# Moving one of seven products behind two other blocks of TensorE work in 19 quads of a gated attention layer

## The reference

```python
x = x + tanh(g_xattn) * attention(layernorm(x), ctx)
n = layernorm(x)                                   # 2048 tokens x 512
scores = softmax(n @ gate_w.T)                     # 64 experts
w_e    = top-8 of scores, the rest 0
flat   = w_e[:, inv_map]                           # 8 groups x 8
scalar = flat.sum(-1)
soft   = softmax(where(flat == 0, -1e9, flat), -1)
xg = n[:, None, :] + einsum('ngi,ghi->ngh', soft, mask_up_w)
g  = einsum('ngh,gih->ngi', xg, gate_proj_w)       # inner size 352 per group
u  = einsum('ngh,gih->ngi', xg, up_proj_w)
d  = einsum('ngi,ghi->ngh', silu(g) * u, down_proj_w)
x  = x + tanh(g_ffn) * einsum('ng,ngh->nh', scalar, d)
```

## Time and profile before

| | us |
|---|---|
| median of 3 runs | 1065.21 |
| lowest and highest of them | 1064.68, 1065.55 |
| the profiled execution | 1064.01 |
| its span in the profile | 1062.2 |

### The profile page before, as it was taken

How to read it: one execution, slowest core, us unless ns; L and a number is a source line. 1 busy time by engine, 2 the same in 40 slices (tenths; PEclk the granted TensorE clock), 3 DMA queues, 4 the chain that set the end, 5 groups by cost and what they waited for, 6 DMA issues and landing times.

```text
span 1062.2 us, 14524 instructions
## 1 busy us (share of the span) xinstructions
PE 1046.7 (99%) x5394; PEld 889.4 (84%) x5394; DVE 747.4 (70%) x1315; ACT 389.5 (37%) x651; POOL 615.6 (58%) x545
## 2 busy tenths in 40 slices
PE   8999999999999999999999999999999999999998
PEld 8889988988988778888887888888888888888887
DVE  7874655676678788788789888765666665666655
ACT  5334324334434434243424342333333333332331
POOL 2112102122435976768878987778668677668661
PEclk9999999999999999999999999999999999999999
DMA  9112225256786314123236332593321211221202
GB/s 335 73 40 99 61 50 149 62 135 144 238 251 198 118 36 56 66 77 35 95 107 81 121 104 97 170 296 114 114 75 48 75 59 44 75 74 48 75 28 80
DMA packets 114277, 111.64 MB, mean 105 GB/s; under 512 B 20896, under 2 KB 96672, under 8 KB 114208
## 3 DMA queue, kind: packets, MB, share of 16 engines
q1 hardware_dynamic: 113840, 110.58, 35.7%
q10 hardware_dynamic: 368, 0.15, 0.1%
HBM read 79.05 MB, written 31.65 MB: 104 GB/s over the span
## 4 chain that ended last, share of the span: by engine, by line
PE 85%; DVE 10%; issue 2%; DMA 1%; ACT 1%; SPq 0%; DVEq 0%
PE bank L84 37%; PE bank L1712 32%; PE bank L1525 8%; PE bank L1718 4%; PE bank L1544 2%; DVE tmp L1364 1%; PE bank L1726 1%; DVE a_stack L1355 1%; DMA wv_raw<-in_w_qkvo 1%; DVE a_tmp L1347 1%; DVE a_stack L1353 1%; DVE tmp L1481 1%; PE bank L1596 1%; DVE tmp L1390 1%; DVE xres L1371 1%
## 5 line engine op out<-in xcount | busy, mean ns | idle before, releaser
L1712 PE MATMUL bank<-x2t,wgu_hi 128*128 128x512 f32 x1144 | 353.0, 390 | 0.0
L665 POOL TENSOR_TENSOR wgu_lo<-wgu_raw,wgu_hi 128x768 fp32r<-128x768 f32 (+2 forms) x143 | 215.4, 1518 | 81.9 <-ACT wgu_hi L818 80.2
L1712 PEld LDWEIGHTS bank<-x2t,wgu_hi 128*128 128x128 f32 x1144 | 214.8, 188 | 44.3
L1712 PE MATMUL bank<-x2t,wgu_lo 128*128 128x512 f32 x572 | 224.3, 392 | 1.1 <-DVE tmp L1422 0.8
L818 ACT CAST wgu_hi<-wgu_raw 128x512 fp32r<-128x512 f32 (+1 forms) x129 | 93.6, 727 | 224.3 <-PE bank L1718 185.3
L1371 DVE TENSOR_TENSOR xres<-xres,bank 128x512 f32<-128x512 f32 x175 | 119.4, 683 | 49.7 <-PE bank L84 49.2
L84 PE MATMUL bank<-wd_hi,at_second 128*128 128x512 f32 x336 | 130.8, 389 | 0.0
L1712 PEld LDWEIGHTS bank<-x2t,wgu_lo 128*128 128x128 f32 x572 | 107.4, 188 | 24.3 <-issue 1.6
L637 POOL TENSOR_TENSOR kt_lo<-ctxt_raw,kt_hi 128x256 fp32r<-128x256 f32 x32 | 23.4, 762 | 138.9 <-ACT kt_hi L826 138.9
L1364 DVE TENSOR_TENSOR tmp<-tmp,scalars 128x512 f32<-128x512 f32 x88 | 101.3, 1151 | 3.3 <-DMA scalars<-scals 0.3
L84 PE MATMUL bank<-wd_hi,at_first 128*128 128x512 f32 x256 | 100.0, 391 | 1.5 <-DVE xres L1371 1.0
(11 more groups left out here) (219 smaller groups left out, 2249.1 us busy)
## 6 DMA issues: line engine op xcount, KB each, us to landing
wgu_raw<-in_w_gate_up SPq DMA_DIRECT2D x43, 512.0 KB, 4.1
wd_raw<-in_w_down SPq DMA_DIRECT2D x22, 512.0 KB, 5.2
a_stacks<-a_stack SPq DMA_DIRECT2D x22, 192.0 KB, 1.9
a_stack<-a_stacks SPq DMA_DIRECT2D x22, 192.0 KB, 4.0
ctxt_raw<-in_ctx_t SPq DMA_DIRECT2D x8, 512.0 KB, 11.3
ctx_raw<-in_ctx SPq DMA_DIRECT2D x8, 512.0 KB, 8.1
x<-x_raw SPq DMA_DIRECT2D x8, 512.0 KB, 8.3
sums_raw<-x SPq DMA_DIRECT2D x16, 256.0 KB, 3.8
```

The source lines that it names most:

```text
L665: last = nc.gpsimd.tensor_tensor(wgu_lo[:, part], raw_of(quad)[:, part], f32(wgu_hi[:, part]), ALU.subtract)
L1712: last = nc.tensor.matmul(out_bank[:], stationary, moving, start=begins and n == 0, stop=n == len(pairs) - 1, skip_group_check=True)
```

## The change

From quad 3 to quad 21 TensorE issues the masked products directly after product 1, and product 6 only after product 2. VectorE issues the mask first and the second sum right behind it, before the other three steps of `a_tile`. ScalarE's rounding of group A waits for product 6 as well, since product 6 now reads its weights later than product 2.

```diff
+def masked_first(q):
+
+    return 2 < q < QUADS // PASSES
 ...
                 if after:
                     eng.wait_ge(s_m2, q + 1)
+                    if masked_first(q):
+                        eng.wait_ge(s_m6, q + 1)
 ...
-            def a_tile(quad):
+            def a_tile(quad, between=None):
+
 ...
                                         columns, ALU.mult).then_inc(s_a_masked, 1)
+                if between is not None:
+                    between(quad)
                 dve.wait_ge(s_a_masked, q + 1)
 ...
                 if q not in (1, 2):
-                    second_sum(quad)
+                    if not masked_first(q):
+                        second_sum(quad)
 ...
                     if quad.first_pass:
-                        a_tile(quad)
+                        a_tile(quad, second_sum if masked_first(q) else None)
 ...
                 product_1(quad)
-                product_6(quad)
+                if not masked_first(q):
+                    product_6(quad)
 ...
                 product_2(quad)
+                if masked_first(q):
+                    product_6(quad)
                 product_5(quad)
```

## The result

| | before | after |
|---|---|---|
| median of the runs, us | 1064.97 (4 runs) | 1104.92 (4 runs, 1102.53 to 1106.37) |
| profiled execution | 1064.01 | 1102.53 |
| its span | 1062.2 | 1100.7 |
| granted clock over the span | 1.0 | 0.995 |

The change makes the kernel slower by a factor of 1.0368 (95% interval 1.0355 to 1.038), 40 us. The forecast was 1091, with a range up to 1101: the direction and the main mechanism were right, and the size was short by 14 us.

A forecast was written before the change was run, and what follows sets the result against it. TensorE, busy 99% of the span, bounds the kernel. Odd-quad stalls 9.6 plus even-quad stalls 22.5 less old stalls 6.0 give 26 us: 1064.0 becomes 1090.1, and the median, 1.2 above, 1091; range 1077 to 1101.

The forecast's parts named there:

- TensorE's list and the old stalls: Time changes only where TensorE stops or gets more work; its old waits for the stack, quads 3 to 21, cost 6.0 us.
- The difference starts at 6.03 instead of 4.33: On VectorE, difference, copy and rest queue behind the second sum, which waits for product 6; over 1.6 us they stall TensorE.
- What three steps cost beside GpSimd: VectorE's difference, copy and rest, met by a GpSimd piece, end about 0.15, 0.22 and 0.41 us after it.
- 9.6 + 22.5: New stalls of the soft products: eight odd quads at 1.2 us, 9.6; nine even quads at 2.5 us, 22.5.
- quad 9: Odd quad where ScalarE is late and GpSimd idles 3.28 us before group A: steps take 1.4 us, no stall.
- Smaller waits: Product 2 on ScalarE's copy and masked products on low weights lose cover: between 0 and 5 us in all, taken as 0.
- Free steps: VectorE's three steps fit in GpSimd's gaps, taking up to 1.6 us, and the old stalls go: 1059 us; chance 0.06.
- The rival above my forecast: Waits on ScalarE's copy and low weights come on top, or most even quads fall as quad 20: 1099 to 1104; chance 0.15.
- even quads like quad 20: GpSimd works without a gap, so VectorE's rest ends at 11.0 us into the quad: a stall of 3.4 us.

## Why the prediction was wrong, by its own steps

- **TensorE's list and the old stalls.** Right. TensorE is still what the time hangs on, and where the old stalls stood (6.0 us) there are now the new ones.
- **The difference starts at 6.03 instead of 4.33.** Right: 5.97 in quad 11, with VectorE idle for 2.43 us in front of the second sum.
- **What three steps cost beside GpSimd.** Right: 0.22 and 0.41 us behind the end of a piece, again. Taking the pieces away made the copy 0.36 us. The stalls came to 30.8 us where the sum had 9.6 + 22.5 = 32.1, but that this is so near is partly luck. The nine even quads stalled by 2.2 us each instead of 2.5 (19.6 in all), and nine odd quads stalled instead of eight (11.2 in all): quad 9, which was to have none, waits 1.1 us. And 7.4 of the 30.8 are there only because the routing waits hold product 6 back, which the prediction did not have.
- **Smaller waits.** This is the step that failed. It named the lost cover of 1.36 us for product 2 and for the masked products' weights, gave both between 0 and 5 us and took 0. The routing products, which stand between the masked products and product 2 in eight quads, it used only to make the even quads' stalls a little smaller; their own wait, for the last addition that VectorE made for the quad before, it put at nothing, and gave no reason. The waits of PEld before the change already had it, in quad 13 and, shorter, in quads 5 and 9 (line 1609):

```profile
PEld bank L1586 <- DVE xres L1371: 1.0, 1, 1.0
PEld bank L1609 <- DVE xres L1371: 0.5, 2, 0.3
```

  This wait grew to 9.1 us in six quads, and since product 6 had moved behind these products, the waits also moved the second sum and the stack behind it. Moving the routing products behind product 6 was worth 20 us, of which some 5 are fewer drops of the clock.
- **The clock.** The prediction had no term for it: it took a stall at its own length. Stalls of about 2 us were followed in some quads by 3.4 us at half clock, 1.7 us each, two times in the stretch in one profile of the changed kernel and four in the next. In three of its four timed executions the mean granted clock was 0.992, which is some 9 us lost over the execution, against 2 at the 0.998 that most executions of the kernel before show. That makes an estimate of where the 14 us went: 8 at the routing products, 7 at the clock, and 1 less at the stack.
- **Rivals.** "Free steps" did not come true, and the gating of GpSimd shows what it would have needed. The rival above my forecast, at 1099 to 1104, came nearest in time, by luck: its reasons were ScalarE's copy, the low weights and even quads like quad 20. TensorE waits for neither of the first two in the changed kernel's stretch, and the even quads lost less than forecast; what came on top was the routing products and the clock.

## What to carry to other kernels

When an instruction is moved from in front of a block to behind it, everything in the block loses its length as cover. Go through every wait inside the block, with what each producer's end is in the latest quad and not in the clean one, and ask what the moved instruction now inherits from those waits.
A short VectorE chain between buffers in SBUF is as long as the GpSimd pieces it meets: look where the pieces lie before moving the chain, and if one must give way, let GpSimd's wait. One line that makes GpSimd wait in ten quads brought 0.5% here, which none of the orders tried on TensorE did.
A stall of about 2 us can cost more than its length, so price the clock beside it.

## What the runs showed of the hardware

- A VectorE copy of 128x384 in SBUF took 0.36 us alone and 1.93 beside a GpSimd subtraction of 1.84 us, ending 0.22 us after it. The GpSimd subtraction kept its 1.84 us. The rule of the Trainium skill that the prediction cited ("SBUF — State Buffer", section "Who interferes with whom"), blocking and not sharing, agrees with these rows and with quad 20's.
- TensorE's clock fell to half for about 3.4 us behind stalls of some 2 us, not behind each of them: quads 6 and 14 in one execution, 5, 8, 10 and 14 in the next. Quad 20's stall (2.7 us idle), the longest, was followed by none in either of these two, but by one in the run with GpSimd's wait in the odd quads. The shortest stall with a drop behind it was 1.84 us idle (quad 4 of that run).
